# Layer-norm statistics of a linear-attention front end: one token tile at a time, or four tiles ahead of their projections

## The chip, the cores and the metric

One Trainium2 chip, all 8 cores. Every core runs the same program on its own slice of the input and no core talks to another. The metric is the device time of the slowest core, in microseconds.

## The reference

```python
xn = layernorm(x)                       # x: 4 sequences x 4096 tokens x 1024, no gain or bias
K  = elu(xn @ Wk + bk) + 1 ; V = xn @ Wv + bv ; Q = elu(xn @ Wq + bq) + 1     # 16 heads of 64
KV = sum over the sequence of K^T V ; Ksum = sum over the sequence of K
attn = (Q KV) / (Q Ksum + 1e-6) @ Wo + bo
y  = layernorm2(z + relu(z @ W1 + b1) @ W2 + b2),  z = layernorm1(xn + attn)
h  = int(xn[:, 0] + xn[:, 1]) mod 8     # routing: experts h and h+1 mod 8, weight 1/2 each
out = x + y + sum over experts of w[e] * (relu(xn @ W1[e] + b1[e]) @ W2[e] + b2[e])
```

The matrix products take bf16 operands; statistics, sums and transposes are fp32.

## The kernel before, in words

Two cores share a sequence of 4096 tokens. Each core computes the results of 2048 tokens of its own, but KV and Ksum need the whole sequence, so each core runs K and V for all 4096 tokens. The phases follow one another with a barrier between them: A (statistics, K, V, KV), a tail of A (routing), the experts (by far the longest), attention and Wo, a layer norm, the dense FFN, a layer norm, the output.

The change touches phase A, `emit_phase_a`. It loops over 32 tiles ("groups" g) of 128 tokens, 0 to 15 of them the core's own. For a group:

- `emit_stats(g)`: SyncE loads the 128 x 1024 fp32 tile into one of two slots of `xtm_a` (512 KB, L292 through the helper `dma`), once the transposes of group g-2 are done. VectorE sums the row (L400) and scales it to minus the mean (L402). ScalarE writes the squared deviations to `elu_a` (L407) and subtracts the mean in place (L409). VectorE sums the squares (L414) and makes the variance (L416). ScalarE then forms the inverse root as exp(-0.5 ln v) (L422, L424), refines it by one Newton step in five one-column instructions (L426 to L434) and normalizes the tile (L436). For an own group it also copies two columns for the routing (L439, L441). The value `evA[g]` of its semaphore tells TensorE that the tile is ready.
- `emit_T(g)`: TensorE waits for `evA[g]` and transposes the tile in two waves of four 128 x 128 blocks (L455), each evacuated and cast by ScalarE (L466) before the next. Then come 16 matmuls for K (L475) with their bias rows (L479), and 16 for V (L487) with theirs (L491).
- `elu_vmax`, `elu_sexp`, `elu_vtail`: VectorE takes max(K, 0) (L505), ScalarE exp(K) (L517), VectorE joins them (L528) and casts V (L534).
- `emit_kv(g)`: TensorE makes the 8 head-pair products K^T V and the sums of K (L548, L551), and VectorE adds them to `kvacc` and `ksacc` (L563 to L565).

Nothing schedules this program. Each engine executes its list in the order in which the Python code appended to it, and waits on semaphores put in by hand. So the order of calls in the loop at the end of `emit_phase_a` is the order of work:

```python
emit_stats(g, mid_v=..elu_vmax(pg)..,
           mid_s=..elu_sexp(pg), elu_vtail(pg)..)
emit_kv(pg)
ek, ev = emit_T(g)
```

The statistics of group g are interleaved with the ELU of group pg = g-1: `mid_v` puts the maximum of g-1 behind the row sum of g on VectorE, `mid_s` puts the exponential of g-1 ahead of the one-column chain of g on ScalarE. While TensorE runs the projections of g-1, the other engines do the statistics of g. `chain` and `vbar` make an engine wait for its own last instruction.

Of the kernel before, what the change touches and what calls it, by code (L numbers as in the profile page):

```python
# [6 lines left out]
F32 = mybir.dt.float32  # L7
BF16 = mybir.dt.bfloat16
# [5 lines left out]
D = 1024  # L14
# [54 lines left out]
class KB:  # L69
    def __init__(self, debug=(), ngl=NG, alim=6, moe_e=NEXP, moe_y=True, gser=False, moe_wb=True, emod=NEXP, hblk=10000):  # L70
# [19 lines left out]
        self.s_lx = [mk("lx0"), mk("lx1")]  # L90
# [69 lines left out]
    def _decl_sbuf(self):  # L160
# [17 lines left out]
        self.xtm_a = sb("xtm_a", [128, 2 * D], F32, TR, 196608)  # L178
        self.ktm = sb("ktm", [128, 2 * D], BF16, TR + 8192, 196608)
        self.vtm = sb("vtm", [128, 2 * D], BF16, TR + 12288, 196608)  # L180
        self.elu_a = sb("elu_a", [128, 2 * D], F32, TR + 16384, 196608)
# [193 lines left out]
    def emit_phase_a(self):  # L375
        ps = self.ps
        NGL = self.ngl
        evT = {}; evKV = {}; evKVmm = {}; evA = {}; evXN = {}
        evK_s = {}; evK_v = {}; evV_v = {}; evDMA = {}
        evXNw = 0  # L380

        def lhs(c, g):
            own = g < NGOWN
            if own:
                return self.xnbf[:, c * TOWN + g * 128:c * TOWN + g * 128 + 128]
            return self.xnp[:, ((g % 2) * KC + c) * 128:((g % 2) * KC + c + 1) * 128]

        def emit_stats(g, mid_v=None, mid_s=None):
            own = g < NGOWN
            par = g % 2  # L390
            xt = self.xtm_a[:, par * D:(par + 1) * D]
            if g >= 2:
                self.wait("Y", self.s_mm, evT[g - 2])
            evDMA[g] = self.dma("Y", xt, self.xs[g * 128:(g + 1) * 128, :], self.s_lx[par])
            mc = self.mstat[:, g:g + 1] if own else self.scol[:, 0:1]
            rc = self.rstat[:, g:g + 1] if own else self.scol[:, 1:2]
            ac = self.scol[:, 2:3]
            sq = self.elu_a[:, par * D:(par + 1) * D]
            self.wait("V", self.s_lx[par], evDMA[g])
            self.em("V", lambda v, xt=xt, mc=mc: v.reduce_sum(mc, xt, axis=AXX))  # L400
            self.vbar()
            self.em("V", lambda v, mc=mc: v.tensor_scalar_mul(mc, mc, -INV_D))  # L402
# [4 lines left out]
            self.em("S", lambda s, xt=xt, sq=sq, mc=mc: s.activation(sq, xt, AF.Square, bias=mc))  # L407
            self.chain("S", self.s_sc)
            self.em("S", lambda s, xt=xt, mc=mc: s.add(xt, xt, mc))  # L409
# [4 lines left out]
            self.em("V", lambda v, sq=sq, ac=ac: v.reduce_sum(ac, sq, axis=AXX))  # L414
            self.vbar()
            self.em("V", lambda v, ac=ac: v.tensor_scalar(ac, ac, INV_D, EPS_LN, op0=OP.mult, op1=OP.add))  # L416
            v_ac = self.inc("V", self.s_ve, 1)
            if mid_s is not None:
                mid_s()
            r0 = self.scol[:, 3:4]  # L420
            self.wait("S", self.s_ve, v_ac)
            self.em("S", lambda s, ac=ac, r0=r0: s.activation(r0, ac, AF.Ln))  # L422
            self.chain("S", self.s_sc)
            self.em("S", lambda s, r0=r0: s.activation(r0, r0, AF.Exp, scale=-0.5))  # L424
            self.chain("S", self.s_sc)
            self.em("S", lambda s, rc=rc, r0=r0: s.mul(rc, r0, r0))  # L426
            self.chain("S", self.s_sc)
            self.em("S", lambda s, rc=rc, ac=ac: s.mul(rc, rc, ac))
            self.chain("S", self.s_sc)
            self.em("S", lambda s, rc=rc: s.mul(rc, rc, self.nwc_sb[:, 0:1]))  # L430
            self.chain("S", self.s_sc)
            self.em("S", lambda s, rc=rc: s.add(rc, rc, self.nwc_sb[:, 1:2]))
            self.chain("S", self.s_sc)
            self.em("S", lambda s, rc=rc, r0=r0: s.mul(rc, rc, r0))  # L434
            self.chain("S", self.s_sc)
            self.em("S", lambda s, xt=xt, rc=rc: s.mul(xt, xt, rc))  # L436
            if own:
                self.chain("S", self.s_sc)
                self.em("S", lambda s, xt=xt, g=g: s.copy(self.xn01[:, g:g + 1], xt[:, 0:1]))  # L439
                self.chain("S", self.s_sc)  # L440
                self.em("S", lambda s, xt=xt, g=g: s.copy(  # L441
                    self.xn01[:, NGOWN + g:NGOWN + g + 1], xt[:, 1:2]))
            evA[g] = self.inc("S", self.s_sc, 1)

        def emit_T(g):
            nonlocal evXNw
            own = g < NGOWN
            par = g % 2
            xt = self.xtm_a[:, par * D:(par + 1) * D]
            self.wait("T", self.s_sc, evA[g])  # L450
            for wave in range(2):
                self.wait("T", self.s_sc, evXNw)
                for j in range(4):
                    c = wave * 4 + j
                    self.em("T", lambda t, xt=xt, c=c, j=j: t.transpose(  # L455
# [6 lines left out]
                if (not own) and g >= 2:  # L462
# [4 lines left out]
                evXNw = self.inc("S", self.s_sc, 1)  # L467
            evXN[g] = evXNw
# [13 lines left out]
            evKmm = self.inc("T", self.s_mm, 1)  # L482
# [12 lines left out]
            evVmm = self.inc("T", self.s_mm, 1)  # L495
            return evKmm, evVmm

        def elu_vmax(g, evKmm):
            par = g % 2
            rt = self.elu_a[:, par * D:(par + 1) * D]  # L500
            self.wait("V", self.s_mm, evKmm)
            if g >= 2:
                self.wait("V", self.s_mm, evKVmm.get(g - 2, 0))
            for hh in range(2):
                self.em("V", lambda v, hh=hh, rt=rt: v.tensor_scalar(  # L505
                    rt[:, hh * 512:(hh + 1) * 512], ps[hh][:], 0.0, None, op0=OP.max))
            evK_v[g] = self.inc("V", self.s_ve, 1)

        def elu_sexp(g, evKmm):
            par = g % 2  # L510
            kslot = self.ktm[:, par * D:(par + 1) * D]
            self.wait("S", self.s_mm, evKmm)
            self.wait("S", self.s_ve, evK_v[g])
            if g >= 2:
                self.wait("S", self.s_mm, evKVmm.get(g - 2, 0))
            for hh in range(2):
                self.em("S", lambda s, hh=hh, kslot=kslot: s.activation(  # L517
                    kslot[:, hh * 512:(hh + 1) * 512], ps[hh][:], AF.Exp))
            evK_s[g] = self.inc("S", self.s_sc, 1)

        def elu_vtail(g, evVmm):
            par = g % 2
            kslot = self.ktm[:, par * D:(par + 1) * D]
            vslot = self.vtm[:, par * D:(par + 1) * D]
            rt = self.elu_a[:, par * D:(par + 1) * D]
            self.wait("V", self.s_sc, evK_s[g])
            for hh in range(2):
                self.em("V", lambda v, hh=hh, kslot=kslot, rt=rt: v.scalar_tensor_tensor(  # L528
                    kslot[:, hh * 512:(hh + 1) * 512], kslot[:, hh * 512:(hh + 1) * 512],
                    1.0, rt[:, hh * 512:(hh + 1) * 512], op0=OP.min, op1=OP.add))  # L530
            self.vbar()
            self.wait("V", self.s_mm, evVmm)
            for hh in range(2):
                self.em("V", lambda v, hh=hh, vslot=vslot: v.tensor_copy(  # L534
                    vslot[:, hh * 512:(hh + 1) * 512], ps[2 + hh][:]))
            evV_v[g] = self.inc("V", self.s_ve, 1)

        def emit_kv(g):
            par = g % 2
            kslot = self.ktm[:, par * D:(par + 1) * D]  # L540
            vslot = self.vtm[:, par * D:(par + 1) * D]
# [3 lines left out]
            for pr in range(NPAIR):  # L545
                b = 5 + pr // 4
                o = pr % 4
                self.em("T", lambda t, pr=pr, b=b, o=o, kslot=kslot, vslot=vslot: t.matmul(  # L548
                    ps[b][:, o * 128:(o + 1) * 128], kslot[:, pr * 128:(pr + 1) * 128],
                    vslot[:, pr * 128:(pr + 1) * 128], start=True, stop=True))  # L550
                self.em("T", lambda t, pr=pr, kslot=kslot: t.matmul(  # L551
# [16 lines left out]
        pend = []  # L568
        for g in range(NGL):
            if pend:  # L570
                pg, ek, ev = pend.pop(0)
                emit_stats(g, mid_v=lambda pg=pg, ek=ek: elu_vmax(pg, ek),
                           mid_s=lambda pg=pg, ek=ek, ev=ev: (elu_sexp(pg, ek),
                                                             elu_vtail(pg, ev)))
                emit_kv(pg)
            else:
                emit_stats(g)
            ek, ev = emit_T(g)
            pend.append((g, ek, ev))
        pg, ek, ev = pend.pop(0)  # L580
        elu_vmax(pg, ek)
        elu_sexp(pg, ek)
        elu_vtail(pg, ev)
        emit_kv(NGL - 1)
# [689 lines left out]
```

How the kernel before makes its waits and increments, by code:

```python
    def wait(self, e, sem, val):  # L242
        if val > 0:
            self.L[e].append(lambda x, s=sem.h, v=val: x.wait_ge(s, v))
            self.meta[e].append(("wait", sem.name, val))
# [4 lines left out]
        def fn(x, prev=prev, s=sem.h, n=n):  # L250
            prev(x).then_inc(s, n)
```

## Time and profile before

| | us |
|---|---|
| median of 4 runs | 5996.84 |
| the four runs | 5885.70, 5881.61, 6531.41, 6107.99 |
| profiled execution, device time | 5886.27 |
| its span, slowest core (core 5) | 5884.7 |
| spans of the 8 cores | 5873.2 to 5884.7 |

The profiled execution is 1.6 us longer than its span, and lies beside the two fastest of the four runs. TensorE is busy for 82% of the span, VectorE for 30%, ScalarE for 18%, GpSimd for 6%. The granted TensorE clock is given as a share of full speed: 1.00 is 2.4 GHz and 0.50 is 1.2 GHz. Phase A begins when the constants have landed and its first row sum starts, and ends with the last addition to `ksacc`.

### The profile page before, as it was taken

How to read it: one execution, taken by the hardware profiler on the slowest of the kernel's cores; microseconds unless marked ns; L12 is line 12 of the kernel's file. 1: busy time of each engine (PE TensorE's matmuls, PEld its weight loads, DVE VectorE, ACT ScalarE, POOL GpSimd, SP SyncE). 2: the span in 40 equal slices, each digit the busy share in tenths (PEclk: the TensorE clock that was granted, in tenths of full speed). 3: DMA queues.
4: the chain of work that ended last, by engine and by line, in shares of the span. 5: the costliest groups of instructions: out<-in, count | busy, mean ns of one | idle time of the engine just before them, and what ended most of it. 6: DMA issues, size and time to landing. Idle time of an engine off the chain costs nothing.

```text
span 5884.7 us, 55904 instructions; the slowest of 8 cores (5873.2 to 5884.7 us)
## 1 busy us (share of the span) xinstructions
PE 4854.7 (82%) x21665; PEld 2130.1 (36%) x21665; DVE 1779.1 (30%) x3367; ACT 1044.6 (18%) x2045; POOL 344.5 (6%) x661
## 2 busy tenths in 40 slices
PE   4777499999999999999999999999975434777722
PEld 2333144444444444444444444444432211333301
DVE  2444222222222222222222222222224254111173
ACT  3444111111111111111111111111102100101100
POOL 1000000000000000000000000000000000000000
PEclk8778799999999999999999999999987666999965
DMA  2000022222222222222222222222212110111103
GB/s 59 29 33 26 15 40 38 36 38 38 36 37 39 35 38 38 36 38 38 36 37 40 37 36 38 40 35 38 38 24 40 45 22 11 26 27 27 25 0 114
DMA packets 105683, 209.47 MB, mean 36 GB/s; under 512 B 12960, under 2 KB 13232, under 8 KB 105424
## 3 DMA queue, kind: packets, MB, share of 16 engines
q0 software_dynamic: 91056, 163.84, 17.8%
q1 hardware_dynamic: 14368, 42.06, 2.2%
q8 instruction: 177, 2.90, 0.2%
q14 instruction: 82, 0.67, 0.0%
HBM read 361.06 MB, written 8.39 MB: 63 GB/s over the span
## 4 chain that ended last, share of the span: by engine, by line
PE 77%; DVE 10%; ACT 5%; DMA 4%; issue 3%; POOL 0%; DVEq 0%; ACTq 0%; SPq 0%; POOLq 0%
PE ps L726 30%; PE ps L764 30%; PE ps L1063 4%; PE ps L1084 4%; PE ps L475 3%; DMA xt_b<-xs 1%; ACT h_b L1073 1%; DMA xtm_b<-xs 1%; PE ps L770 1%; PE ps L455 1%; DVE x_sb L1101 1%; DVE ln_t L1031 1%; DVE ln_t L1029 1%; PE ps L947 1%; DVE acc L788 1%
## 5 line engine op out<-in xcount | busy, mean ns | idle before, releaser
L726 PE MATMUL ps<-xnbf,w1s 128*128 128x512 bf16 x8192 | 1825.7, 381 | 53.7 <-DVE wb L711 32.3
L726 PEld LDWEIGHTS ps<-xnbf,w1s 128*128 128x128 bf16 x8192 | 799.5, 98 | 1046.5 <-issue 105.9
L764 PE MATMUL ps<-h_hi,w2s 128*128 128x512 bf16 x4096 | 923.6, 384 | 22.5 <-DVE acc L788 22.5
L764 PE MATMUL ps<-h_lo,w2s 128*128 128x512 bf16 x4096 | 904.9, 379 | 0.0
L788 DVE TENSOR_TENSOR acc<-acc,ps 128x512 f32<-128x512 f32 x992 | 614.8, 681 | 835.7 <-PE ps L764 533.4
L764 PEld LDWEIGHTS ps<-h_hi,w2s 128*128 128x128 bf16 x4096 | 404.6, 99 | 521.9 <-issue 51.5
L736 ACT ACTIVATE h_lo<-ps,eb_sb 128x512 bf16<-128x512 f32 x512 | 310.2, 688 | 1542.0 <-PE ps L726 1542.0
L764 PEld LDWEIGHTS ps<-h_lo,w2s 128*128 128x128 bf16 x4096 | 400.8, 98 | 483.3
L736 ACT ACTIVATE h_hi<-ps,eb_sb 128x512 bf16<-128x512 f32 x512 | 310.2, 688 | 1461.4 <-PE ps L726 1461.4
L744 DVE TENSOR_TENSOR h_lo<-h_lo,wb 128x512 bf16<-128x512 bf16 x512 | 183.2, 419 | 949.0 <-ACT h_lo L736 949.0
L744 DVE TENSOR_TENSOR h_hi<-h_hi,wb 128x512 bf16<-128x512 bf16 x512 | 183.1, 419 | 898.6 <-ACT h_hi L736 898.6
L1063 PE MATMUL ps<-c_bf,w1s 128*128 128x512 bf16 x1024 | 243.2, 399 | 103.3 <-ACT h_b L1073 75.8
L1084 PE MATMUL ps<-h_b,w2s 128*128 128x512 bf16 x1024 | 238.9, 394 | 91.2 <-DVE x_sb L1101 58.8
L292 POOL DMA_DIRECT2D w2s<-ew_pk x256 | 135.1, 528 | 1736.4 <-PE ps L764 1187.3
L292 POOL DMA_DIRECT2D w1s<-ew_pk x256 | 135.3, 529 | 1691.0 <-PE ps L726 1691.0
L1063 PEld LDWEIGHTS ps<-c_bf,w1s 128*128 128x128 bf16 x1024 | 102.2, 102 | 245.0 <-issue 141.1
L1101 DVE TENSOR_TENSOR x_sb<-x_sb,ps 128x512 f32<-128x512 f32 x96 | 59.5, 681 | 421.2 <-PE ps L1084 421.2
L1084 PEld LDWEIGHTS ps<-h_b,w2s 128*128 128x128 bf16 x1024 | 100.8, 101 | 229.3 <-issue 123.1
L985 PE MATMUL ps<-ln_bf,onescol_bf 128*1 128x512 bf16 x64 | 33.2, 519 | 167.1 <-DVE ln_bf L980 167.1
L1073 ACT ACTIVATE h_b<-ps,b_sb 128x512 bf16<-128x512 f32 x128 | 77.5, 688 | 526.3 <-PE ps L1063 526.3
L455 PE MATMUL ps<-ident,xtm_a 128*128 128x128 f32 x256 | 58.3, 370 | 99.7 <-ACT xn L441 61.6
L926 PE MATMUL ps<-ident,xt_b 128*128 128x128 f32 x128 | 34.8, 427 | 111.8 <-DVE xt_b L918 111.8
(178 smaller groups left out, 2258.6 us busy)
## 6 DMA issues: line engine op xcount, KB each, us to landing
w1s<-ew_pk POOLq DMA_DIRECT2D x256, 256.0 KB, 3.5
w2s<-ew_pk POOLq DMA_DIRECT2D x256, 256.0 KB, 3.5
xtm_a<-xs SPq DMA_DIRECT2D x32, 512.0 KB, 3.3
xt_b<-xs SPq DMA_DIRECT2D x32, 256.0 KB, 2.6
w1s<-w_pk POOLq DMA_DIRECT2D x32, 256.0 KB, 3.5
w2s<-w_pk POOLq DMA_DIRECT2D x32, 256.0 KB, 3.5
xtm_b<-xs SPq DMA_DIRECT2D x16, 512.0 KB, 4.2
out<-otm_b SPq DMA_DIRECT2D x16, 512.0 KB, 2.9
```

The source lines that it names most:

```text
L292: self.em(e, lambda x, o=out, i=in_: x.dma_start(out=o, in_=i))
L455: self.em("T", lambda t, xt=xt, c=c, j=j: t.transpose(ps[4][:, j * 128:(j + 1) * 128], xt[:, c * 128:(c + 1) * 128], self.ident[:]))
L475: self.em("T", lambda t, k=k, hh=hh, lh=lhs(k, g): t.matmul(ps[hh][:], lh, self.wk_sb[:, k * D + hh * 512:k * D + (hh + 1) * 512], start=( ...
L726: self.em("T", lambda t, k=k, tt=tt, slot=slot: t.matmul(ps[tt][:], self.w1t(slot, k), self.xnbf[:, k * TOWN + tt * 512:k * TOWN + (tt + 1 ...
L736: self.em("S", lambda s, tt=tt, i=i, hreg=hreg, e=e, n=n: s.activation(hreg[:, i * TOWN + tt * 512:i * TOWN + (tt + 1) * 512], ps[tt][:], ...
L744: self.em("V", lambda v, tt=tt, i=i, hreg=hreg, e=e: v.tensor_mul(hreg[:, i * TOWN + tt * 512:i * TOWN + (tt + 1) * 512], hreg[:, i * TOWN ...
L764: self.em("T", lambda t, j=j, tt=tt, slot=slot, hreg=hreg, lp=last_plain: t.matmul(ps[4 + tt][:], self.w2t(slot, j), hreg[:, j * TOWN + tt ...
L788: self.em("V", lambda v, dst=dst, tt=tt: v.tensor_add(dst, dst, ps[4 + tt][:]))
L1063: self.em("T", lambda t, k=k, tt=tt, slot=slot: t.matmul(ps[tt][:], self.w1t(slot, k), self.c_bf[:, k * TOWN + tt * 512:k * TOWN + (tt + 1 ...
L1073: self.em("S", lambda s, tt=tt, i=i, n=n: s.activation(self.h_b2[:, i * TOWN + tt * 512:i * TOWN + (tt + 1) * 512], ps[tt][:], AF.Relu, bi ...
L1084: self.em("T", lambda t, j=j, tt=tt, slot=slot: t.matmul(ps[4 + tt][:], self.w2t(slot, j), self.h_b2[:, j * TOWN + tt * 512:j * TOWN + (tt ...
L1101: self.em("V", lambda v, x=xsl, tt=tt: v.tensor_add(x, x, ps[4 + tt][:]))
```

## The change

The 32 groups are treated in 8 batches of four. For a batch, `stats_sums` runs for all four groups, one after the other, then `stats_finish` forms the four inverse roots together on 128 x 4 columns and normalizes the four tiles. Only then come transposes, projections, ELU and K^T V, group by group. `xtm_a` has four slots instead of two (its neighbours in memory move up), with four load semaphores, and a load waits for the transposes of group g-4. The Newton step moves from five ScalarE instructions per group to four VectorE instructions per batch. An own group gets one more VectorE copy (of the mean, L416 of the kernel after) and one more ScalarE copy (of the inverse deviation, L449 of the kernel after). The instructions of transposes, projections, ELU and K^T V, their waits among one another and their order within a group stay as they were.

```diff
-        self.xtm_a = sb("xtm_a", [128, 2 * D], F32, TR, 196608)
+        self.xtm_a = sb("xtm_a", [128, 4 * D], F32, TR, 196608)
...
-        def emit_stats(g, mid_v=None, mid_s=None):
+        def stats_sums(g, j):
...
+            if g >= 4:
+                self.wait("Y", self.s_mm, evT[g - 4])
+            evDMA[g] = self.dma("Y", xt, self.xs[g * 128:(g + 1) * 128, :], self.s_lx[g % 4])
...
+            self.wait("V", self.s_lx[g % 4], evDMA[g])
+            self.em("V", lambda v: v.reduce_sum(mc, xt, axis=AXX))
+            self.vbar()
+            self.em("V", lambda v: v.tensor_scalar_mul(mc, mc, -INV_D))
+            v_negm = self.inc("V", self.s_ve, 1)
+            self.wait("S", self.s_ve, v_negm)
...
+            self.em("S", lambda s: s.activation(sq, xt, AF.Square, bias=mc))
             self.chain("S", self.s_sc)
+            self.em("S", lambda s: s.add(xt, xt, mc))
             s_sub = self.inc("S", self.s_sc, 1)
-            if mid_v is not None:
-                mid_v()
             self.wait("V", self.s_sc, s_sub)
+            self.em("V", lambda v: v.reduce_sum(ac, sq, axis=AXX))
+            self.vbar()
+            if own:
+                mm_dst = self.mstat[:, g:g + 1]
+                self.em("V", lambda v: v.tensor_copy(mm_dst, mc))
+                self.vbar()
+
+        def stats_finish(gs):
...
+            self.em("V", lambda v: v.tensor_scalar(a, a, INV_D, EPS_LN, op0=OP.mult, op1=OP.add))
...
+            self.em("S", lambda s: s.activation(r0, a, AF.Ln))
+            self.chain("S", self.s_sc)
+            self.em("S", lambda s: s.activation(r0, r0, AF.Exp, scale=-0.5))
...
+            self.em("V", lambda v: v.tensor_mul(rcb, r0, r0))
...
+            self.em("V", lambda v: v.tensor_mul(rcb, rcb, a))
...
+            self.em("V", lambda v: v.tensor_scalar(rcb, rcb, -0.5, 1.5, op0=OP.mult, op1=OP.add))
...
+            self.em("V", lambda v: v.tensor_mul(rcb, rcb, r0))
...
+            for j, g in enumerate(gs):
...
+                self.em("S", lambda s, xt=xt, rc=rc: s.mul(xt, xt, rc))
...
-        pend = []
-        for g in range(NGL):
...
+        nb = NGL // 4
+        for b in range(nb):
+            gs = [4 * b + j for j in range(4)]
+            for j, g in enumerate(gs):
+                stats_sums(g, j)
+            stats_finish(gs)
+            for g in gs:
+                emit_trans(g)
+                emit_proj(g)
+                elu_vmax(g)
+                elu_sexp(g)
+                elu_vtail(g)
+                emit_kv(g)
```

VectorE, an own group in the middle of phase A, before. L505, L528 and L534 are the ELU and the cast of group g-1, L563 to L565 its sums; the row sum L400 and the sum of squares L414 are of group g.

```order
L400 TENSOR_REDUCE mstat<-xtm_a 128x1
L402 TENSOR_SCALAR mstat<-mstat 128x1
L505 TENSOR_SCALAR elu_a<-ps 128x512 x2
L414 TENSOR_REDUCE scol<-elu_a 128x1
L416 TENSOR_SCALAR scol<-scol 128x1
L528 SCALAR_TENSOR_TENSOR ktm<-ktm,elu_a 128x512 x2
L534 CAST vtm<-ps 128x512 x2
L563 TENSOR_TENSOR kvacc<-kvacc,ps 128x512
L564 TENSOR_TENSOR kvacc<-kvacc,ps 128x512
L565 TENSOR_TENSOR ksacc<-ksacc,ps 128x8
```

VectorE after, the last group of the statistics of a batch and the first ELU behind it. L400 to L416 stand there four times in a row (once shown), L464 to L573 four times behind them (once shown).

```order
L400 TENSOR_REDUCE scol<-xtm_a 128x1
L402 TENSOR_SCALAR scol<-scol 128x1
L412 TENSOR_REDUCE tpack<-elu_a 128x1
L416 COPY mstat<-scol 128x1
L424 TENSOR_SCALAR tpack<-tpack 128x4
L432 TENSOR_TENSOR scol<-tpack 128x4
L434 TENSOR_TENSOR scol<-scol,tpack 128x4
L436 TENSOR_SCALAR scol<-scol 128x4
L438 TENSOR_TENSOR scol<-scol,tpack 128x4
L464 TENSOR_SCALAR elu_a<-ps 128x512 x2
L485 SCALAR_TENSOR_TENSOR ktm<-ktm,elu_a 128x512 x2
L491 CAST vtm<-ps 128x512 x2
```

The statistics no longer stand between the pieces of an ELU: all of a batch stand ahead of its first ELU, and behind the last sums of the batch before.

ScalarE at the same place of the order, before, from the exponential of group g-1 to the casts of the transposes of group g:

```order
L517 ACTIVATE ktm<-ps 128x512 x2
L422 ACTIVATE scol<-scol 128x1
L424 ACTIVATE scol<-scol 128x1
L426 ACTIVATE rstat<-scol 128x1
L428 ACTIVATE rstat<-rstat,scol 128x1
L430 ACTIVATE rstat<-rstat,nwc_sb 128x1
L432 ACTIVATE rstat<-rstat,nwc_sb 128x1
L434 ACTIVATE rstat<-rstat,scol 128x1
L436 ACTIVATE xtm_a<-xtm_a,rstat 128x1024
L439 COPY xn_106<-xtm_a 128x1
L441 COPY xn_106<-xtm_a 128x1
L466 CAST xnbf<-ps 128x128 x8
```

ScalarE after, in a batch of groups that are not the core's own, from the last squares (L407) to the casts of the second group (L514); L446 normalizes the tiles, L475 is the exponential:

```order
L407 ACTIVATE elu_a<-xtm_a,scol 128x1024
L409 ACTIVATE xtm_a<-xtm_a,scol 128x1024
L427 ACTIVATE tpack<-tpack 128x4
L429 ACTIVATE tpack<-tpack 128x4
L446 ACTIVATE xtm_a<-xtm_a,scol 128x1024 x4
L514 CAST xnp<-ps 128x128 x8
L475 ACTIVATE ktm<-ps 128x512 x2
L514 CAST xnp<-ps 128x128 x8
```

The first casts of a batch stand behind all four normalizations, and between two later groups ScalarE has only the exponential and the casts.

## Rows read from the trace of the kernel before

**Rows 1.** Busy time by stretch: until phase A starts, and phase A.

```profile
core 5: us, PE busy (x) PEld busy (x) DVE busy (x) ACT busy (x) POOL busy (x), PEclk, DMA share, GB/s
0.00:38.47 38.47, 0.00 (x0) 0.00 (x0) 0.97 (x3) 0.00 (x0) 18.88 (x40) 1.00 0.89 142
38.47:604.66 566.19, 407.62 (x1920) 177.16 (x1920) 247.96 (x417) 258.75 (x673) 0.00 (x0) 0.80 0.09 28
```

**Rows 2.** Groups of instructions in phase A: busy, mean ns, idle before, releaser.

```profile
L475 PE MATMUL ps<-wk_sb,xnp 128*128 128x512 bf16 x256 | 87.8, 518 | 20.7 <-ACT xnp L466 20.7
...
L487 PE MATMUL ps<-wv_sb,xnp 128*128 128x512 bf16 x256 | 58.0, 380 | 0.0
...
L505 DVE TENSOR_SCALAR elu_a<-ps 128x512 f32<-128x512 f32 x64 | 41.2, 685 | 259.4 <-PE ps L479 259.4
```

**Rows 3.** The transposes, L455: what their engine waited for (us, times).

```profile
  ACT xn L441: 61.6, 16
...
  ACT xtm_a L436: 5.0, 15
```

**Rows 4.** Timeline, group 0: start, length, engine, line, out<-in, count [idle before].

```profile
38.47 1.16 DVE L400 TENSOR_REDUCE mstat<-xtm_a 128x1 f32<-128x1024 f32 x1
39.73 0.15 DVE L402 TENSOR_SCALAR mstat<-mstat 128x1 f32<-128x1 f32 x1
39.97 1.28 ACT L407 ACT_TABLE_LOAD   x1 [39.97 <-DVE mstat L402]
41.26 1.15 ACT L407 ACTIVATE elu_a<-xtm_a,mstat 128x1024 f32<-128x1024 f32 x1
...
43.75 1.22 DVE L414 TENSOR_REDUCE scol<-elu_a 128x1 f32<-128x1024 f32 x1 [3.86 <-ACT xtm_a L409]
45.07 0.15 DVE L416 TENSOR_SCALAR scol<-scol 128x1 f32<-128x1 f32 x1
...
45.32 0.20 ACT L422 ACTIVATE scol<-scol 128x1 f32<-128x1 f32 x1 [1.67 <-DVE scol L416]
45.62 0.20 ACT L424 ACTIVATE scol<-scol 128x1 f32<-128x1 f32 x1
...
47.84 1.15 ACT L436 ACTIVATE xtm_a<-xtm_a,rstat 128x1024 f32<-128x1024 f32 x1
49.08 0.19 ACT L439 COPY xn<-xtm_a 128x1 f32<-128x1 f32 x1
49.36 0.19 ACT L441 COPY xn<-xtm_a 128x1 f32<-128x1 f32 x1
...
49.69 1.09 PE L455 MATMUL ps<-ident,xtm_a 128*128 128x128 f32 x4 [49.69 <-ACT xn L441]
50.87 0.77 ACT L466 CAST xnbf<-ps 128x128 bf16<-128x128 f32 x4 [1.32 <-PE ps L455]
```

**Rows 5.** Timeline, the seam between groups 15 and 16.

```profile
330.95 0.69 DVE L563 TENSOR_TENSOR kvacc<-kvacc,ps 128x512 f32<-128x512 f32 x1 [1.22 <-PE ps L551]
331.05 0.63 PE L455 MATMUL ps<-ident,xtm_a 128*128 128x128 f32 x4 [0.28 <-ACT xtm_a L436]
...
332.23 1.21 DVE L400 TENSOR_REDUCE scol<-xtm_a 128x1 f32<-128x1024 f32 x1
```

**Rows 6.** The chain that ended last, in order of time: K projections of groups 0, 4, 14.

```profile
53.88 5.90 PE ps L475 x16
...
124.20 6.57 PE ps L475 x16
...
301.47 5.00 PE ps L475 x16
```

**Rows 7.** DMA in the first 60 us, the queue of the tile loads: packets, MB, share.

```profile
q1 hardware_dynamic: 432, 1.57, 9.3%
```

**Rows 8.** The chain that ended last: the last constant, issued by GpSimd.

```profile
19.34 17.81 DMA nwc_sb<-nwc_c
```

**Rows 9.** The tile loads in the whole trace.

```profile
DMA to landing us min/median/max: 3.1/3.3/6.6
```

More of the change, by code:

```diff
@@ L377, in emit_phase_a @@
         NGL = self.ngl
+        assert NGL % 4 == 0
         evT = {}; evKV = {}; evKVmm = {}; evA = {}; evXN = {}
         evK_s = {}; evK_v = {}; evV_v = {}; evDMA = {}
-        evXNw = 0
+        evKmm = {}; evVmm = {}
+        evXNw = [0]
         def lhs(c, g):
-            own = g < NGOWN
-            if own:
+            if g < NGOWN:
                 return self.xnbf[:, c * TOWN + g * 128:c * TOWN + g * 128 + 128]
             return self.xnp[:, ((g % 2) * KC + c) * 128:((g % 2) * KC + c + 1) * 128]
-        def emit_stats(g, mid_v=None, mid_s=None):
+        def stats_sums(g, j):
             own = g < NGOWN
[L390 to L400, printed above, removed]
+            sl = g % 4
+            xt = self.xtm_a[:, sl * D:(sl + 1) * D]
+            if g >= 4:
+                self.wait("Y", self.s_mm, evT[g - 4])
+            evDMA[g] = self.dma("Y", xt, self.xs[g * 128:(g + 1) * 128, :], self.s_lx[g % 4])
+            mc = self.scol[:, j:j + 1]
+            ac = self.tpack[:, j:j + 1]
+            sq = self.elu_a[:, (g % 2) * D:(g % 2 + 1) * D]
+            self.wait("V", self.s_lx[g % 4], evDMA[g])
+            self.em("V", lambda v: v.reduce_sum(mc, xt, axis=AXX))
             self.vbar()
-            self.em("V", lambda v, mc=mc: v.tensor_scalar_mul(mc, mc, -INV_D))
+            self.em("V", lambda v: v.tensor_scalar_mul(mc, mc, -INV_D))
             v_negm = self.inc("V", self.s_ve, 1)
@@ L413, in emit_stats @@
             self.wait("V", self.s_sc, s_sub)
-            self.em("V", lambda v, sq=sq, ac=ac: v.reduce_sum(ac, sq, axis=AXX))
+            self.em("V", lambda v: v.reduce_sum(ac, sq, axis=AXX))
             self.vbar()
-            self.em("V", lambda v, ac=ac: v.tensor_scalar(ac, ac, INV_D, EPS_LN, op0=OP.mult, op1=OP.add))
+            if own:
[3 more added lines that the diff above has]
+        def stats_finish(gs):
+            nb = len(gs)
+            a = self.tpack[:, 0:nb]
+            r0 = self.tpack[:, 4:4 + nb]
+            rcb = self.scol[:, 0:nb]
+            self.em("V", lambda v: v.tensor_scalar(a, a, INV_D, EPS_LN, op0=OP.mult, op1=OP.add))
@@ L427, in emit_stats @@
[L427 to L436, printed above, removed]
@@ L437, in emit_stats @@
-            if own:
-                self.chain("S", self.s_sc)
[L439 to L449, printed above, removed]
+            self.em("S", lambda s: s.activation(r0, r0, AF.Exp, scale=-0.5))
@@ new lines, in stats_finish @@
+            s_r0 = self.inc("S", self.s_sc, 1)
+            self.wait("V", self.s_sc, s_r0)
+            self.em("V", lambda v: v.tensor_mul(rcb, r0, r0))
[3 more added lines that the diff above has]
+            self.em("V", lambda v: v.tensor_scalar(rcb, rcb, -0.5, 1.5, op0=OP.mult, op1=OP.add))
+            self.vbar()
+            self.em("V", lambda v: v.tensor_mul(rcb, rcb, r0))
+            v_rcb = self.inc("V", self.s_ve, 1)
@@ new lines, in stats_finish @@
+            self.wait("S", self.s_ve, v_rcb)
+            for j, g in enumerate(gs):
+                own = g < NGOWN
+                sl = g % 4
+                xt = self.xtm_a[:, sl * D:(sl + 1) * D]
+                rc = rcb[:, j:j + 1]
+                self.em("S", lambda s, xt=xt, rc=rc: s.mul(xt, xt, rc))
+                self.chain("S", self.s_sc)
+                if own:
+                    self.em("S", lambda s, rr=self.rstat[:, g:g + 1], rc=rc: s.copy(rr, rc))
+                    self.chain("S", self.s_sc)
+                    self.em("S", lambda s, xt=xt, g=g: s.copy(self.xn01[:, g:g + 1], xt[:, 0:1]))
+                    self.chain("S", self.s_sc)
+                    self.em("S", lambda s, xt=xt, g=g: s.copy(
+                        self.xn01[:, NGOWN + g:NGOWN + g + 1], xt[:, 1:2]))
+                    self.chain("S", self.s_sc)
+                evA[g] = self.s_sc.n
@@ new lines, in elu_vmax, with elu_sexp @@
+        def elu_vmax(g):
+            rt = self.elu_a[:, (g % 2) * D:(g % 2 + 1) * D]
+            self.wait("V", self.s_mm, evKmm[g])
+            if g >= 2:
+                self.wait("V", self.s_mm, evKVmm.get(g - 2, 0))
+            for hh in range(2):
+                self.em("V", lambda v, hh=hh: v.tensor_scalar(
+                    rt[:, hh * 512:(hh + 1) * 512], ps[hh][:], 0.0, None, op0=OP.max))
+            evK_v[g] = self.inc("V", self.s_ve, 1)
+        def elu_sexp(g):
+            kslot = self.ktm[:, (g % 2) * D:(g % 2 + 1) * D]
+            self.wait("S", self.s_mm, evKmm[g])
+            self.wait("S", self.s_ve, evK_v[g])
+            if g >= 2:
+                self.wait("S", self.s_mm, evKVmm.get(g - 2, 0))
+            for hh in range(2):
+                self.em("S", lambda s, hh=hh: s.activation(
+                    kslot[:, hh * 512:(hh + 1) * 512], ps[hh][:], AF.Exp))
+            evK_s[g] = self.inc("S", self.s_sc, 1)
@@ new lines, in elu_vtail @@
+        def elu_vtail(g):
+            kslot = self.ktm[:, (g % 2) * D:(g % 2 + 1) * D]
+            vslot = self.vtm[:, (g % 2) * D:(g % 2 + 1) * D]
+            rt = self.elu_a[:, (g % 2) * D:(g % 2 + 1) * D]
+            self.wait("V", self.s_sc, evK_s[g])
+            for hh in range(2):
+                self.em("V", lambda v, hh=hh: v.scalar_tensor_tensor(
+                    kslot[:, hh * 512:(hh + 1) * 512], kslot[:, hh * 512:(hh + 1) * 512],
+                    1.0, rt[:, hh * 512:(hh + 1) * 512], op0=OP.min, op1=OP.add))
+            self.vbar()
+            self.wait("V", self.s_mm, evVmm[g])
+            for hh in range(2):
+                self.em("V", lambda v, hh=hh: v.tensor_copy(
+                    vslot[:, hh * 512:(hh + 1) * 512], ps[2 + hh][:]))
+            evV_v[g] = self.inc("V", self.s_ve, 1)
@@ L450, in emit_T, with emit_trans @@
+        def emit_trans(g):
+            sl = g % 4
+            xt = self.xtm_a[:, sl * D:(sl + 1) * D]
             self.wait("T", self.s_sc, evA[g])
             for wave in range(2):
-                self.wait("T", self.s_sc, evXNw)
+                self.wait("T", self.s_sc, evXNw[0])
                 for j in range(4):
                     c = wave * 4 + j
-                    self.em("T", lambda t, xt=xt, c=c, j=j: t.transpose(
+                    self.em("T", lambda t, c=c, j=j: t.transpose(
@@ L461, in emit_T @@
                 self.wait("S", self.s_mm, mmv)
-                if (not own) and g >= 2:
+                if (g >= NGOWN) and g >= 2:
                     self.wait("S", self.s_mm, evKVmm.get(g - 2, 0))
@@ L466, in emit_T, with emit_proj @@
                     self.em("S", lambda s, dst=lhs(c, g), j=j: s.copy(dst, ps[4][:, j * 128:(j + 1) * 128]))
-                evXNw = self.inc("S", self.s_sc, 1)
-            evXN[g] = evXNw
+                evXNw[0] = self.inc("S", self.s_sc, 1)
+            evXN[g] = evXNw[0]
+        def emit_proj(g):
             self.wait("T", self.s_sc, evXN[g])
@@ L494, in emit_T @@
                     start=False, stop=True))
[L495 to L536, printed above, removed]
+            evVmm[g] = self.inc("T", self.s_mm, 1)
@@ L538, in emit_kv @@
         def emit_kv(g):
-            par = g % 2
-            kslot = self.ktm[:, par * D:(par + 1) * D]
-            vslot = self.vtm[:, par * D:(par + 1) * D]
+            kslot = self.ktm[:, (g % 2) * D:(g % 2 + 1) * D]
+            vslot = self.vtm[:, (g % 2) * D:(g % 2 + 1) * D]
             self.wait("T", self.s_ve, evV_v[g])
```

38 lines of the change are left out of this document (7 added, 31 removed).

## The prediction

> **What bounds the kernel now.** I read the stretches first. Phase A runs from 38.47 to 604.66 us, 566.19 us for 32 groups, 17.7 us each, at a mean granted clock of 0.80 [rows 1]. Nothing behind phase A is touched by the change, so the question is what these 566 us become, and what happens to the load ahead of them.
>
> Inside phase A the groups of instructions show two loops that feed each other [rows 2]. TensorE does the K projection, then V. VectorE sits idle for 259.4 us in front of L505, waiting for the end of K. So VectorE and ScalarE have room, and the statistics of the next tile are done in that room.
>
> The third view is what TensorE waits for in front of its transposes, since that is where late statistics would show [rows 3]. For own groups it is the routing copies behind the normalized tile, 61.6 us in 16 waits. The first of these is the start of the kernel, 49.69 us [rows 4], so the other 15 are worth 11.9 us. For the other groups it is the normalization itself, 5.0 us in 15 waits. Together 16.9 us, about half a microsecond per group. This is all that the statistics cost beside TensorE's own sequence. The one-column chain L422 to L434 is long (45.32 to 47.84, 2.5 us, in group 0), but it runs beside the cast of V and the K^T V products of the group before, which end nearly as late.
>
> **The change part by part.** All durations are from the profiled execution, 5886.27 us with a span of 5884.7. The median of the runs shown, 5996.84, lies 110.6 us above it.
>
> Part 1, the statistics leave the room beside TensorE. The order shows it. The first row sum of a batch (L400) stands behind the last `ksacc` addition of the batch before, the first ELU stands behind `stats_finish`, and ScalarE casts no transpose before it has normalized all four tiles. TensorE has nothing to do until those casts: only the first wave of transposes can run ahead. I call this stretch the head of a batch. It has three pieces.
>
> Sums of one group: from the row sum to the scaled mean 1.26 us (38.47 to 39.73), to the squares 0.24 (39.73 to 39.97, where the one table load stands, once in either kernel), squares and subtraction 2.49 (41.26 to 43.75), sum of squares 1.32 (43.75 to 45.07) [rows 4]. Sum 5.31 us. An own group adds the copy of the mean, a one-column instruction of 0.15 us with the 0.10 us that lie between the end of one dependent VectorE instruction and the next (39.63 to 39.73 [rows 4]), so 5.56. There is no overlap between two groups, because VectorE's sum of squares waits for ScalarE and the next row sum is queued behind it. Four groups: 22.2 us own, 21.2 us others.
>
> Finish: variance to logarithm 0.25 (45.07 to 45.32), to the exponential 0.30 (45.32 to 45.62), exponential to VectorE 0.30 (0.20 and a handover of 0.10), four small VectorE instructions at 0.25, the last counted to ScalarE's start, 1.00 [rows 4]. The trace has no instruction of 128 x 4; its nearest rows are the one-column ones, and I take their duration. Sum 1.85 us.
>
> Normalization: 1.24 us per tile (47.84 to 49.08), and for an own tile three copies at 0.28 (49.08 to 49.36) [rows 4]. Four tiles: 8.3 us own, 5.0 us others.
>
> A head is thus 32.4 us for an own batch and 28.1 us for another. At the seam the first row sum starts 1.28 us after the first `kvacc` addition (330.95 to 332.23), where without a head TensorE would start the transposes about 0.2 us before that addition (331.05 less its wait of 0.28 [rows 5]) and ScalarE the casts 1.18 us later (49.69 to 50.87 [rows 4]). The seam therefore costs the head plus 0.3 us: 32.7 and 28.4. The first batch has no seam. There the casts start 32.4 + 1.28 for the table load = 33.7 us after the first row sum instead of 12.4 (38.47 to 50.87 [rows 4]): 21.3 us more. In all 21.3 + 3 x 32.7 + 4 x 28.4 = 233.0 us.
>
> Part 2, what the change gives back. With the tiles ready, the waits in front of the transposes go: 16.9 us [rows 3]. What is late next is the end of the K^T V products on TensorE itself, so no more comes of it. The seven small ScalarE instructions per group fall to two per batch, but that only shortens what lies in the head already.
>
> Part 3, the clock. TensorE's K projection has 16 matmuls. In phase A K is busy for 87.8 us in 16 groups, 5.5 us each, V 3.6 us [rows 2]. K starts at 1.2 GHz and ends at 2.4; the same number of columns takes V a third less. After the idle 49.69 us at the start, K of group 0 took 5.90 us; the longest took 6.57, a short one 5.00 [rows 6]. Group 0 stands for the first group of every batch, so 8 x 0.4 = 3 us, and I take 4 with the second wave of transposes. From the longest row it would be 8 x 1.1 = 9 us. It could also be a gain: groups 1 to 3 of a batch follow each other half a microsecond closer, and if all K were as short as 5.00 us, 31 x 0.5 = 15 us would go.
>
> The Trainium skill weighs against the change here. Its page "TensorE: Matmul & The Clock Gate", section "HAM oscillation", says that a kernel which idles TensorE between bursts starts every burst at the low clock, and restructuring for unbroken work was worth 1.7 times there. By that rule each head would be followed by a cold start that the kernel before does not have. The trace agrees only in part: K of every group shown begins slow already, with gaps of a few microseconds only, so the rule's price here is the difference of rows above, 3 to 9 us, and no multiple.
>
> Part 4, the loads. Four tiles instead of two are asked for at the start, on engines that are 0.89 busy with the weights [rows 1], and VectorE and ScalarE wait for the last constant, issued at 19.34 and landed 17.81 us later [rows 8]. Three tile loads (1.57 MB) take 9.3% of the engines' first 60 us [rows 7], that is 1.9 us each, so two more cost 3.7 us. Bounds: nothing if they fill the unused tenth, 13 us if each costs the longest landing of 6.6 us [rows 9]. Later loads are issued three groups or more ahead and land in 3.3 us, hidden.
>
> Sum: 233.0 - 16.9 + 4 + 3.7 = 223.8 us. 5886.3 + 223.8 = **6110 us**, 3.8% slower. A measurement of this kernel can tell about 2% from no change, here 118 us.
>
> **The rivals.**
> *Heads are hidden.* If the statistics of the next batch ran beside TensorE's work on the last groups of this one, the seven later heads (213 us) would shrink to nothing, and with them all hidden the time would be 5886.3 + 223.8 - 213 = 5897, no change. For it: VectorE idles for 259.4 us [rows 2], more than the heads need, and the tiles are loaded in time. Against it: the order of the lists, which no engine leaves here. It decides once 15 us of each of the seven heads are hidden (7 x 15 = 105, leaving 119). Chance 0.04.
> *The clock stays up inside a batch.* If the shorter gaps let K run like V, 5.5 - 3.6 = 1.9 us in 24 groups go, 45 us: 6065. Against it: the order inside a group is the same, and the seam shrinks by half a microsecond only. Chance 0.06.
> *The clock stays down for all of a batch's first group.* K 6.6 instead of 5.5, and V as slow as K: 1.1 + 3 us, eight times, 33 us more than nothing, 29 more than I took: 6139. Chance 0.12.
> *Only the small instructions matter.* If the one-column chain alone set the pace of a group, its removal would give back 32 x 2.5 = 80 us instead of 16.9: 6047. Against it: TensorE waited only 16.9 us for it. Chance 0.05.
>
> **How the numbers follow.** My forecast, with its own range of 6085 to 6130 from the bounds above (loads 0 to 13, clock -15 to 9, and a few us for the 128 x 4 instructions), has 0.73; the rivals have 0.04, 0.06, 0.12 and 0.05. The range goes down to 6070, just above the second rival. Upwards it takes in the third rival and, since the numbers shown for the kernel before have a median 110.6 us above the execution that I count from, the same sum made from that median, 5996.84 + 223.8 = 6221: the top is 6225. Of the chances, slower by over 2% (above 6004) has my forecast and three rivals, 0.95 with a little taken off for an error in the sum; within 2% has 0.04 to 0.05; faster by over 2% would need heads hidden and the clock up together, 0.01.
>
> **What would show it.** In the trace after, phase A should last some 785 us: eight stretches of about 28 to 34 us in which TensorE does at most four transposes, ended by ScalarE's casts; between them groups of about 17 us. TensorE's wait in front of the transposes should be nil inside a batch and some 25 us or more at its first group. VectorE should show the chain L400, L402, L412 four times at 5.3 to 5.6 us. The expert phase should be as long as before. I am wrong if row sums of a batch start before the last `kvacc` addition of the batch before, if a head is under 20 us, or if the groups inside a batch take less than 16 us.

## The result and the profile after

The changed kernel runs in 6109.09 us, median of 7 runs (lowest 6100.14); the kernel before in 5886.22, median of 10. The ratio is 1.0376, 95% interval 1.0363 to 1.039: slower by 3.8%. The profiled execution of after took 6101.35 us, 215.1 more than that of before. In some executions of any kernel here the cores of one die (0 to 3 or 4 to 7) or of both run at a lower granted clock and end later; ratios leave these out, medians do not, and of the profiles of e2, e5 and e7, which are such executions, only cores 0 to 3 (e2, e5) or the first 70 us (e7) are quoted.

Busy time by stretch of after, as [rows 1]:

```profile
0.00:41.44 41.44, 0.00 (x0) 0.00 (x0) 0.97 (x3) 0.00 (x0) 18.87 (x40) 1.00 0.90 157
41.44:825.02 783.58, 392.06 (x1889) 173.93 (x1920) 258.58 (x441) 208.10 (x481) 0.00 (x0) 0.74 0.06 19
825.02:6099.80 5274.78, 4421.31 (x19357) 1952.49 (x19745) 1530.23 (x2949) 784.92 (x1372) 325.57 (x621) 0.92 0.21 36
```

Phase A lasts 783.6 us instead of 566.2, and starts 3.0 us later. That is 220.4 us. Behind it lie 5274.8 us against 5280.0 (5884.7 - 604.7), 5 us in the other direction, less than the 12 us by which the cores of one run differ.

What TensorE waited for in front of the transposes, as [rows 3], and VectorE in front of the ELU, as [rows 2]:

```profile
  ACT xn L453: 155.0, 4
  ACT xtm_a L446: 106.9, 4
```

```profile
L464 DVE TENSOR_SCALAR elu_a<-ps 128x512 f32<-128x512 f32 x64 | 41.2, 685 | 332.9 <-PE ps L529 332.9
```

Before, TensorE waited for a tile 31 times, apart from the first for half a microsecond each. Now there are eight such waits, the first of them the start of the kernel (69.50 us), the others 27 to 29 us long: one per batch. The waits for a tile inside the batches are gone; those for the cast between the two waves of a tile are in either kernel. VectorE waits even longer for the end of K than before (332.9 us, was 259.4), so the room in which the statistics used to be done is still there and is now empty.

Timeline of after, the head of the second batch:

```profile
142.35 1.21 DVE L400 TENSOR_REDUCE scol<-xtm_a 128x1 f32<-128x1024 f32 x1
143.67 0.15 DVE L402 TENSOR_SCALAR scol<-scol 128x1 f32<-128x1 f32 x1
143.97 1.15 ACT L407 ACTIVATE elu_a<-xtm_a,scol 128x1024 f32<-128x1024 f32 x1 [6.97 <-DVE scol L402]
145.21 1.15 ACT L409 ACTIVATE xtm_a<-xtm_a,scol 128x1024 f32<-128x1024 f32 x1
146.46 1.22 DVE L412 TENSOR_REDUCE tpack<-elu_a 128x1 f32<-128x1024 f32 x1 [2.64 <-ACT xtm_a L409]
147.78 0.15 DVE L416 COPY mstat<-scol 128x1 f32<-128x1 f32 x1
148.11 1.22 DVE L400 TENSOR_REDUCE scol<-xtm_a 128x1 f32<-128x1024 f32 x1 [0.17 <-DVE mstat L416]
...
165.24 0.17 DVE L424 TENSOR_SCALAR tpack<-tpack 128x4 f32<-128x4 f32 x1
...
167.17 1.15 ACT L446 ACTIVATE xtm_a<-xtm_a,scol 128x1024 f32<-128x1024 f32 x1 [1.17 <-DVE scol L438]
...
169.41 1.09 PE L503 MATMUL ps<-ident,xtm_a 128*128 128x128 f32 x4 [28.51 <-ACT xn L453]
...
175.51 0.77 ACT L514 CAST xnbf<-ps 128x128 bf16<-128x128 f32 x4
176.43 1.09 PE L503 MATMUL ps<-ident,xtm_a 128*128 128x128 f32 x4 [5.94 <-ACT xnbf L514]
```

VectorE and ScalarE take turns. Each group of sums is 5.76 us (142.35 to 148.11), four of them 22.9, the finish 1.93 (165.24 to 167.17), the four normalizations with their copies 8.3 (to 175.51). TensorE sits idle for 28.51 us, does one wave of transposes, and sits idle for another 5.94.

### The profile page after: what moved, and what is told of

Its sections match the earlier page's. It is cut to its first block, busy times and chain, and to the rows that moved or that the text cites. A ratio compares the mean times of both kernels' runs of the same rounds, so it can differ in the third digit from the quotient of the medians.

```text
span 6099.8 us, 55163 instructions; the slowest of 8 cores (6091.2 to 6099.8 us)
## 1 busy us (share of the span) xinstructions
PE 4813.4 (79%) x21246; PEld 2126.4 (35%) x21665; DVE 1789.8 (29%) x3391; ACT 993.0 (16%) x1853; POOL 344.4 (6%) x661
## 4 chain that ended last, share of the span: by engine, by line
PE 74%; DVE 12%; ACT 6%; DMA 4%; issue 3%; DVEq 0%; POOL 0%; ACTq 0%; SPq 0%; POOLq 0%
PE ps L730 29%; PE ps L768 29%; PE ps L1067 4%; PE ps L1088 4%; PE ps L525 3%; DMA xt_b<-xs 1%; ACT h_b L1077 1%; DMA xtm_b<-xs 1%; PE ps L774 1%; DVE x_sb L1105 1%; DVE ln_t L1033 1%; DVE ln_t L1035 1%; PE ps L503 1%; DVE vtm L491 1%; DVE ktm L485 1%
## 5 line engine op out<-in xcount | busy, mean ns | idle before, releaser
L768 PE MATMUL ps<-h_hi,w2s 128*128 128x512 bf16 x4008 | 917.4, 384 | 27.6 <-DVE acc L792 22.9
L503 PEld LDWEIGHTS ps<-ident,xtm_a 128*128 128x128 f32 x256 | 35.3, 174 | 333.5 <-issue 333.5
```

The costliest lines, as they stand in the source:

```text
L503: self.em("T", lambda t, c=c, j=j: t.transpose(ps[4][:, j * 128:(j + 1) * 128], xt[:, c * 128:(c + 1) * 128], self.ident[:]))
L768: self.em("T", lambda t, j=j, tt=tt, slot=slot, hreg=hreg, lp=last_plain: t.matmul(ps[4 + tt][:], self.w2t(slot, j), hreg[:, j * TOWN + tt ...
```

## The experiments

**e1, the sums of two groups overlapped inside a head.**

```diff
-            for j, g in enumerate(gs):
-                stats_sums(g, j)
+            for j, part in ((0, 0), (1, 0), (0, 1), (2, 0), (1, 1), (3, 0), (2, 1), (3, 1)):
+                stats_sums(gs[j], j, part)    # part 1: only the sum of squares
```

> The changed kernel with one edit: inside a head the row sum of the next group goes ahead of the sum of squares of this one, on VectorE. Theory A (a head is a serial chain that bounces between VectorE and ScalarE, all of it exposed): VectorE's part of a group is 2.9 to 3.2 us and ScalarE's 2.5, so four groups of sums take about 14.5 us instead of 22.8, 8 us less in each of 8 heads, about 66 us: some 6035 us (6020 to 6050), ratio to before 1.025. Theory B (TensorE is held up by something else in the head, such as the clock or the order of the casts): no change from 6100 to 6110.

Lowest 6046.61 us, ratio 1.0255 (1.0177 to 1.0333), spans 6038.9 to 6045.7: theory A. From the profiled execution of after to that of e1 it is 54 us, not the 66 expected. The heads did get 66 us shorter in sum; K took 5 us longer over the 32 groups, and 6 us more lie behind phase A, less than the cores of one run differ. The timeline of e1 (L410 and L412 are the row sum and the mean, L402 the sum of squares, L417 the squares) shows the two engines side by side; the next group follows after 3.1 us instead of 5.8:

```profile
139.06 1.22 DVE L410 TENSOR_REDUCE scol<-xtm_a 128x1 f32<-128x1024 f32 x1 [0.17 <-DVE mstat L406]
140.38 0.15 DVE L412 TENSOR_SCALAR scol<-scol 128x1 f32<-128x1 f32 x1
140.49 1.22 DVE L402 TENSOR_REDUCE tpack<-elu_a 128x1 f32<-128x1024 f32 x1
140.63 1.15 ACT L417 ACTIVATE elu_a<-xtm_a,scol 128x1024 f32<-128x1024 f32 x1 [1.04 <-DVE scol L412]
...
142.13 1.22 DVE L410 TENSOR_REDUCE scol<-xtm_a 128x1 f32<-128x1024 f32 x1 [0.17 <-DVE mstat L406]
```

**e2, the Newton step per group again, inside the head.** The batched Ln, Exp and four VectorE instructions are replaced by the seven one-column ScalarE instructions of before, four times.

> The changed kernel with the batched Newton step undone: per group the seven one-column ScalarE instructions of before, inside the head. Theory A (everything in a head is exposed): four chains of 2.5 us instead of one of 1.7, 8.4 us per head, 67 us in all: about 6168 us. Theory B (short instructions are hidden in either order, as they were before, where TensorE waited 16.9 us for the statistics in all): within 15 us of the changed kernel's 6105.

Lowest 6181.19 us, 80 us above the profiled execution of after (6101.35). In the profile cores 0 to 3 took 6166.9 to 6173.3 us, against 6091.2 to 6097.8 in after, 76 us more. Theory A, somewhat more than the 67 expected. So the batching does save these 76 to 80 us, but only as against doing the same work in a head. In the kernel before that work cost little: it lay beside TensorE, whose waits for the statistics came to 16.9 us in all.

**e3, the sums of the next batch between the ELU pieces of this one.**

```diff
+                if nxt:
+                    stats_sums(g + 4, j, 0)      # row sum, VectorE
                 elu_vmax(g)
                 elu_sexp(g)
+                if nxt:
+                    stats_sums(g + 4, j, 1)      # squares, ScalarE
                 elu_vtail(g)
+                if nxt:
+                    stats_sums(g + 4, j, 2)      # sum of squares, VectorE
```

> The changed kernel, but the sums of batch b+1 are put between the ELU pieces of the groups of batch b; only the finish and the four normalizations stay in the head. Theory A (the order alone makes the heads cost what they do): later heads cost 10.7 us own and 7.4 others over a plain seam instead of 33 and 29; with the first batch (+22), the loads (+3) and about 20 us given back at the other seams the time is about 5955 us (5940 to 5975), ratio 1.012. Theory B (the sums were only cheap because one group's worth stood between two groups; VectorE and ScalarE delay the ELU by about 2.5 us in each of 28 groups): about 6020 us.

Median 5954.63 us of 9 runs, ratio 1.0102 (1.0065 to 1.0139): theory A. The same instructions, batches and slots as after, placed beside TensorE's work (the squares use the other half of `elu_a`, so that the ELU of the same moment keeps its own), and some 150 us of the 223 are gone. A later head costs 10.3 us own and 7.4 others over the seam of before, where 10.7 and 7.4 were expected. TensorE's waits in front of the transposes, first the start of the kernel (70.0) with three others, then four:

```profile
  ACT xn L455: 88.1, 4
...
  ACT xtm_a L448: 19.8, 4
```

**e4, no batches, statistics two groups ahead.** The kernel before with the four slots; the loop now calls `emit_stats(g + 2)` around the ELU of g.

> The kernel before, with the four tile slots of the change, and the statistics run two groups ahead of the transposes instead of one; no batches. Theory A (the 16.9 us of waits in front of the transposes are all that the statistics cost before): TensorE's wait for the normalized tile goes to nil, 17 to 20 us less, and a few us more where shorter gaps keep the clock up through a K projection: 5860 us (5850 to 5870), ratio 0.9955. Theory B (ScalarE's order holds the casts back, so the wait only moves from the transposes to the casts): 5880 to 5890.

Its two lowest runs took 5859.43 and 5859.18 us, 27 less than before, with no interval to give; e8 builds on it and has one. Phase A, from its first row sum to its last addition, lasts 534.6 us in e4 and 536.3 in e8, against 566.2 before. TensorE's waits for ScalarE in front of the transposes in e4 are the start and the casts between waves, nothing else:

```profile
  ACT xn L441: 54.1, 1
  ACT xnp L465: 17.0, 16
  ACT xnbf L465: 16.3, 16
```

**e5 and e6, batches of two and of one.** `nb = NGL // 2` (or `// 1`), and so for `gs`.

> The changed kernel with 16 batches of two. Theory A (a head costs its own chain, nearly all of it per group): two groups of sums, one finish, two normalizations: 17.8 us own, 15.6 others, against 33.1 and 28.9 for four. Over the 32 groups that is 23 us more, and a few us of clock: about 6128 us (6115 to 6140). Theory B (what costs is the interruption of TensorE as such, 27 us for each of 8): 8 more interruptions, 216 us more: about 6320.

> The changed kernel with 32 batches of one: no batching at all, but also nothing interleaved. Theory A: 11.1 us own and 10.0 others for each head: about 99 us more than batches of four, about 6205 us (6190 to 6225). Theory B (interruptions as such): 24 more at 27 us, about 6750.

e5: lowest 6126.36 us, 25 more than the profiled execution of after; in the profile cores 0 to 3 took 6108.2 to 6127.7 us, some 24 more. e6: 6221.06 us, ratio 1.0562 (1.0517 to 1.0608). Theory A both times; 32 interruptions cost 116 us more than 8 (6217.48 against 6101.35, the profiled executions), under a fifth of what interruptions as such would (648). A head is paid nearly all by the group, not by the head. In e6 no transpose was short any more; in the listing of its transposes the shortest is 417 ns, where after and before have 272:

```profile
L503 PE MATMUL ps<-ident,xtm_a x256: 417/421/448, 52.3 to 920.0; 128*128 128x128 f32 x128
```

**e7, the loads of tiles 2 and 3 held back.**

```diff
+            if g == 2:
+                self.wait("Y", self.s_aux, self.aux_tgt)
```

> The changed kernel, but the loads of tiles 2 and 3 wait until the constants have landed. Theory A (two more tile loads at the start compete with the weights for the DMA engines): the last constant lands near 37.2 us after its issue began the trace, as before, not 40.1; the first row sum starts at 38.5 instead of 41.4 us, and the first head is as long as it was (34.4 us to the first casts). Theory B (the later start is chance or has another cause): it stays near 41.4.

The last constant in after and in e7, from the chain of waits (start, length):

```profile
19.34 20.78 DMA nwc_sb<-nwc_c
```

```profile
19.34 17.30 DMA nwc_sb<-nwc_c
```

The first row sum starts at 37.96 us on core 4, where after has 41.44: theory A. The first transposes follow 28.1 us later in both (66.03; 69.50 in after). The later loads made no head longer. The start is no accident of one core: the first row sum lies between 40.8 and 43.2 us on all cores of after and of e1 to e6, between 37.7 and 39.0 on all cores of before and of e7 to e10. In the whole time the 3 us do not show: in two other executions of e7 cores 0 to 3 took 6092.4 to 6096.0 us and cores 4 to 7 6083.6 to 6100.6, where after has 6091.2 to 6099.8.

**e8, e9, e10, looking for a version that beats both.** e8 is e4 with the edit of e7. e9 and e10 add matmuls whose result nobody reads, into banks that are idle there:

```diff
+        def filler(n, bank):
+            for _ in range(n):
+                self.em("T", lambda t: t.matmul(
+                    ps[bank][:], self.wk_sb[:, 0:128], self.wv_sb[:, 0:512],
+                    start=True, stop=True))
...
         def emit_kv(g):
+            filler(6, 4)                 # e9 and e10
...
                 if wave == 1:
                     evT[g] = mmv
+                if g >= 1:
+                    filler(2, 0)         # e10 only, behind each wave
```

> e4 (statistics two groups ahead) with the loads of tiles 2 and 3 held back until the constants have landed, as in e7. Expected from e4 and e7 together: phase A starts at about 38 instead of 43 us and is as long as in e4: 5855 us (5848 to 5862), ratio 0.9945. If the gain of e4 was chance of one execution, the ratio is 1.000.

> e8 plus six matmuls per group that compute nothing that is used (128x512, into the idle bank of the transposes), in TensorE's wait of about 1.7 us between V and the K^T V products. They test whether the low clock at the start of each K projection comes from the gaps. Theory A (it does, and this gap is the one that counts): K takes 3.4 us in nearly all groups instead of 5.1 on average, about 50 us less: 5805 us. Theory B (the gaps at the transposes bring the clock down as well): K stays near 5 us, 5850 to 5860. If the six matmuls run late, at the low clock, they cost up to 0.3 us a group: 5865.

> e9 plus two such matmuls behind each wave of transposes (into a K bank that is free there), in the waits of about 1 us for ScalarE's casts. Theory A (gaps bring the clock down): K at 3.4 us and the transposes at their short 272 ns throughout: 5795 to 5805 us. Theory B (the clock at the start of K does not hang on these gaps): as e8, 5855, or up to 20 us more for the added work.

e8: lowest 5848.92 us, ratio 0.9936 (0.9914 to 0.9959). e9: lowest 5816.45, median 5819.60, ratio 0.9884 (0.9862 to 0.9907). e10: lowest 5791.99, ratio 0.9874 (0.9799 to 0.995). All are faster than before, by less than 2% but with intervals that end below 1, and the gain of e4 was no chance. Four rows of the chain of e8, groups that follow each other, and then two of e10; each is a K projection:

```profile
204.87 6.06 PE ps L476 x16
...
221.43 3.61 PE ps L476 x16
...
235.94 5.88 PE ps L476 x16
...
252.47 6.15 PE ps L476 x16
```

```profile
215.21 3.61 PE ps L478 x16
...
229.32 3.61 PE ps L478 x16
```

The same stretch of phase A by windows, e8 first and e10 behind it (the clock is the third number from the end):

```profile
100.00:550.00 450.00, 336.93 (x1679) 144.57 (x1678) 214.92 (x363) 222.78 (x582) 0.00 (x0) 0.85 0.09 30
```

```profile
100.00:550.00 450.00, 359.50 (x2025) 159.66 (x2025) 234.91 (x454) 222.28 (x579) 0.00 (x0) 0.96 0.10 30
```

TensorE's waits in front of the K^T V products (idle before, the last columns), e8 first and e10 behind it:

```profile
L549 PE MATMUL ps<-vtm,ktm 128*128 128x128 bf16 x256 | 25.9, 219 | 57.8 <-DVE vtm L535 57.8
```

```profile
L558 PE MATMUL ps<-vtm,ktm 128*128 128x128 bf16 x256 | 25.5, 218 | 13.7 <-DVE vtm L537 13.7
```

In e8 K switches between two lengths, 3.6 and about 6 us, from group to group. In e10, with the waits filled, the groups are 14.1 us apart and each of the seven K projections that start between 200 and 300 us takes 3.61 us; of all 32 only that of group 0 is longer (5.75). So the low clock at the start of K comes from the waits around it, though the filled ones are mostly about 1.7 us long and shorter (2.1 in two groups, 3.7 in group 0, in e8). e9 lies between: filling the wait in front of the K^T V products alone brings most K projections up, not all. Its lowest run was 5816 where I had expected 5805, so the gaps at the transposes count too. The 3.4 us for K in the expectations of e9 and e10 came from rows of after in which one matmul is not recorded (see below); with all 16 it is 3.61.

## Why the prediction was right

The forecast was 6110 us and 3.8%; measured were 6109.09 and 3.76%. The forecast was added up from profiled executions, and from one profiled execution to the other the increase is 215.1 us, not 223.8: like for like it was 8.7 us too high, and that the median came within a microsecond is luck.

One thing comes ahead of the steps. The trace of after has 1889 of 1920 matmuls in phase A. The 31 missing ones are the first of each K projection but the first: 15 of 16 are recorded, though all 16 weight loads are, and the first recorded matmul starts 0.41 us behind the first weight load instead of 0.03. Group 4 of after, and group 1 of before:

```profile
178.71 0.14 PEld L525 LDWEIGHTS ps<-wk_sb,xnbf 128*128 128x128 bf16 x2 [1.59 <-issue]
179.12 5.77 PE L525 MATMUL ps<-wk_sb,xnbf 128*128 128x512 bf16 x15 [1.60 <-ACT xnbf L514]
```

```profile
71.62 0.14 PEld L475 LDWEIGHTS ps<-wk_sb,xnbf 128*128 128x128 bf16 x2 [1.62 <-issue]
71.65 5.55 PE L475 MATMUL ps<-wk_sb,xnbf 128*128 128x512 bf16 x16 [1.25 <-ACT xnbf L466]
```

So in after I count the start of K from 0.03 us behind its first weight load. That is an estimate of where the missing matmul began. By steps:

- **The heads** (233.0 us). First to last, confirmed and a little short. The first batch casts 34.4 us after its first row sum (41.44 to 75.82), predicted 33.7. Between the end of one batch's K^T V products and the next K projection lie 37.8 us in own batches and 33.7 in the others, where before had 5.0 and 4.5: 32.8 and 29.2 more, predicted 32.7 and 28.4. In sum 22 + 3 x 32.8 + 4 x 29.2 = 237. The error is in the small times: a group of sums takes 5.76 us instead of 5.56, because the row sum takes 1.21 us and not 1.16, its scaled mean reaches ScalarE up to 0.06 us later, and the next row sum starts 0.33 us after the start of the copy of the mean and not 0.25. That all of it is exposed is shown by e1, e2, e3, e5 and e6, each within its expected range or some us beside it.
- **What comes back** (16.9 us). Inside the batches the seam between K^T V and the next K shrank from 4.92 to 3.55 us in own groups and from 4.35 to 3.83 in the others, 23 us over 24 seams. That is more than the waits that went. Of the 192 transposes in these seams 51 took over 400 ns, where before had 112, which is 8 us.
- **The clock** (+4 us). From K's start to the end of K^T V all groups together took 3 us more, all of it in K: 5.6 us on average instead of 5.5. Both of the things that I had weighed against each other are in this number. In four groups inside the batches (6, 9, 13 and 21) the clock stayed up through all of K (3.40 us for 15 matmuls, third row below, 3.6 for 16), and in most others K was longer than before, up to 6.3 us. In the chain of after:

```profile
179.12 5.77 PE ps L525 x15
196.19 5.76 PE ps L525 x15
212.66 3.40 PE ps L525 x15
227.24 5.60 PE ps L525 x15
```

- **The loads** (+3.7 us). Measured 2.97 (37.15 to 40.12 us for the last constant), and e7 gives it back at the start.
- **The sum.** 237 - 23 + 3 + 3 = 220 us in phase A and ahead of it, predicted 224, and 5 us the other way behind it. The forecast had four us too little for the heads and six too little for what comes back; these work against each other in the sum, so that it is closer than its terms is again partly luck. The mechanism is not.

Of the rivals, hidden heads are refuted by the trace (VectorE's first row sum of a batch starts only behind the `ksacc` addition) and built on purpose in e3. (The prediction prices seven heads at 213 us; its own terms give 3 x 32.7 + 4 x 28.4 = 211.7.) The clock that stays up was real but small here, in four groups of 24. Those four took 14.4 us each, less than the 16 us that the prediction names as a sign of being wrong; the other groups inside the batches took 16.0 to 18.3, and what the sign stood for, a gain of some 45 us, did not come. The clock that stays down through a batch's first group did not occur: first groups have K of 4.9 to 6.4 us, as others do, and V of 3.63. Nor did the small instructions set the pace of a group: 23 us came back, not 80. After a head's idle time K took 5.76 us on average and 5.52 in the other groups of after, some 2 us in all. The Trainium skill ("TensorE: Matmul & The Clock Gate", "HAM oscillation") says that a kernel which lets TensorE idle between bursts starts every burst at the low clock. The trace agrees, but K starts low in nearly all groups without a head too (20 of 24), so the rule had almost no price here. What both kernels lose to the low clock in K is lost at the short gaps that are in both, and those are what e10 shows to be worth some 57 us (5848.92 to 5791.99).

## What to carry to other kernels

Count a batched step in what stands exposed, not in instructions: 28 short ScalarE instructions per batch became six, two on ScalarE and four on VectorE, which saved 76 to 80 us against the same work in the same place, and the place cost over 200. With in-order engines and hand-written waits, work is hidden only if it stands between two pieces of the list that wait anyway, so look ahead by slots (e4, e8) rather than in blocks. And where waits of one or two microseconds recur between matmuls, try to fill them before shortening anything else: useless matmuls took 32 us (e9) and 57 us (e10) off e8, by the lowest runs, where the better place of the statistics (e4) had brought 27.

## What was not expected of the hardware

Waits of one to two microseconds, several per group of 17 us, were enough in the kernel before to bring TensorE to 1.2 GHz for the first part of every K projection (at least 4.9 us, against 3.6 for V); ten filler matmuls per group, some 2 us of work, raised the granted clock of the stretch from 0.85 to 0.96 and shortened each group to 14.1 us. And holding back two loads of 512 KB at the start lets the weights and constants land about 3 us sooner, though DMA was 0.89 to 0.90 busy already. And a trace can lack the same record in nearly every group (the first matmul of K, in after, e3, e4 and e9), which puts each start read from it 0.2 to 0.4 us too late, enough to turn the sign of a small term; the weight loads beside it show this.
